# The softplus of a selective scan as one activation, and three of eight products with C on GpSimd

## What is computed

```
x, z = split(hidden @ W_in)                        # 1024 + 1024 features
x = silu(causal_conv4(x) + conv_b)
x_dbl = x @ W_x                                    # 64 + 16 + 16 columns: dt_raw, B, C
dt = softplus(x_dbl[..., :64] @ W_dt + b_dt)       # 224 x 1024 per sequence
h[t] = exp(dt[t] * A) * h[t-1] + (dt[t] * x[t]) * B[t]      # 16 states per feature
y[t] = sum over the 16 states of h[t] * C[t]
y = (y + x * D) * silu(z);  out = residual + y @ W_out
```

## Time and profile before

| | us |
|---|---|
| median of 3 runs (3502.21 to 3515.01) | 3507.85 |
| profiled execution, first to last instruction | 3514.3 |
| PE busy | 3186.9 (91%) |
| DVE busy | 2650.7 (75%) |
| ACT busy | 2396.1 (68%) |
| POOL busy | 1805.3 (51%) |

### The profile page before, as it was taken

One profiled execution on the slowest core, in us unless ns is written; L12 is line 12 of the kernel. 1 busy time (PEld: TensorE's weight loads), 2 busy tenths in 40 slices (PEclk: granted clock), 3 DMA queues, 4 the chain that ended last, 5 costly groups with the idle time before them and its releaser, 6 DMA issues. The chain is left out here.

```text
span 3514.3 us, 59833 instructions
## 1 busy us (share of the span) xinstructions
PE 3186.9 (91%) x20864; PEld 2223.5 (63%) x20864; DVE 2650.7 (75%) x4673; ACT 2396.1 (68%) x5339; POOL 1805.3 (51%) x1211
## 2 busy tenths in 40 slices
PE   5699889888889888988998899999999999899999
PEld 4566556665566556655665566666666666578887
DVE  2889999999999999999987576777777777523222
ACT  5778887778787887778774477776777677632222
POOL 2677887888787878888786100100000010055554
PEclk8899999999999999999999999999999999999999
DMA  5566666766677666666576121211211121120010
GB/s 164 154 180 183 185 167 164 199 185 163 156 193 192 164 161 184 177 183 158 157 201 182 53 71 49 83 55 47 75 64 47 52 81 66 43 77 25 27 46 24
DMA packets 286298, 425.03 MB, mean 121 GB/s; under 512 B 28753, under 2 KB 226129, under 8 KB 281394
## 3 DMA queue, kind: packets, MB, share of 16 engines
q1 hardware_dynamic: 278637, 411.44, 42.0%
q10 hardware_dynamic: 7365, 9.77, 1.0%
HBM read 320.12 MB, written 101.02 MB: 120 GB/s over the span
## 5 line engine op out<-in xcount | busy, mean ns | idle before, releaser
L811 POOL TENSOR_TENSOR a_hs<-a_rep,a_bmat 128x896 f32<-128x896 f32 x512 | 1061.5, 2097 | 294.6 <-PE a_yps L323 294.4
L443 ACT ACTIVATE a_states<-a_rep,a_a_neg 128x224 f32<-128x224 f32 x2048 | 793.7, 438 | 98.0 <-DVE a_hs L707 96.4
L700 DVE TENSOR_TENSOR_SCAN a_states<-a_states,a_hs 128x900 f32<-128x900 f32 x384 | 779.7, 2031 | 73.8 <-ACT a_states L443 58.5
L1424 DVE CUSTOM_DVE_ANT_0 b_sc<-sps,early_mask 112x375 f32<-112x375 f32 x1024 | 500.3, 545 | 171.7 <-PE sps L1171 162.1
L1311 ACT ACTIVATE b_sc<-b_sc,b_nmax 112x750 f32<-112x750 f32 x512 | 467.3, 913 | 2.5 <-DVE b_nmax L1430 2.5
L1185 PEld LDWEIGHTS b_tps<-ident,b_sc 112*125 112x125 f32 x3072 | 362.2, 191 | 157.4 <-issue 126.1
L1564 POOL TENSOR_SCALAR b_x_var<-mv 112x2 f32<-112x2 f32 x16 | 3.4, 214 | 857.4 <-DVE mv L1475 857.4
L345 PE MATMUL a_work<-early_scan_hT,w_in 128*128 128x224 f32 x2048 | 427.6, 364 | 10.0 <-issue 7.2
L345 PEld LDWEIGHTS a_work<-early_scan_hT,w_in 128*128 128x128 f32 x2048 | 397.9, 197 | 51.1 <-issue 43.4
L707 DVE TENSOR_TENSOR a_hs<-a_states,a_cmat 128x896 f32<-128x896 f32 x384 | 419.2, 1092 | 13.2
L1185 PE MATMUL b_tps<-ident,b_sc 112*125 112x112 f32 x3072 | 410.7, 283 | 16.3 <-DVE b_pT L1438 14.9
(11 more groups left out here) (199 smaller groups left out, 5012.4 us busy)
## 6 DMA issues: line engine op xcount, KB each, us to landing
a_rep<-du_scratch SPq DMA_DIRECT2D x512, 224.0 KB, 5.7
w_in<-W_in_dram SPq DMA_DIRECT2D x128, 512.0 KB, 4.4
du_scratch<-early_du SPq DMA_DIRECT2D x16, 1792.0 KB, 11.4
ctx<-ctxT_dram SPq DMA_DIRECT2D x48, 500.0 KB, 5.8
v_scratch<-kv_out SPq DMA_DIRECT2D x96, 250.0 KB
k_scratch<-kv_out SPq DMA_DIRECT2D x96, 250.0 KB, 4.4
b_keys<-k_scratch SPq DMA_DIRECT2D x8, 1500.0 KB, 9.2
b_v<-v_scratch SPq DMA_DIRECT2D x8, 1500.0 KB
```

Of the source, the lines that this page charges most:

```text
L443: e = act.activation(rows(states[:, g % DA, :])[:, q, 1:ROW], rep[tile % REPS][:, j, 0, :], ACT.Exp, scale=a_neg[:, g % SLOTS, q:q + 1])
L700: dve.tensor_tensor_scan(state if g % G4 else whole, state, whole, 0.0, ALU.mult, ALU.add).then_inc(S["scan"], 1)
L811: pool.tensor_tensor(hs[g % RING][:, :, 1:ROW], rep[tile % REPS][:, j, 1, :].unsqueeze(1).broadcast_to([P, Q, L]), bmat[b % 2][:], ALU.mul ...
L1424: dve.tensor_tensor_reduce(out=sc[buffer_of(block)][:, j, cols], in0=sps[0:TT, j, 0:HALF], in1=mask[:, block % 2, cols], scale=-1.0, scala ...
```

## The change

The softplus becomes one Softplus activation per pair of tiles, straight from PSUM into dt. VectorE's two passes, GpSimd's sum and six of the seven activation passes are gone. Softplus is in a table of its own, so the four activations stand together in one slot with a table load before and after them. GpSimd makes the product with C for three slots of eight (g % 8 of 0, 4 and 6) and VectorE for five; before it was two and six. The tables of slots move with it: the dt matmuls of a sequence in two pairs, at slots 18 and 21, the softplus at 21, `scale_x` at 22, `store_du` at 23, z one slot later, some of the key and value units shifted. `skip` no longer stands behind the softplus.

```diff
-            "silu_x": [-43], "x_dbl": [-42], "xd": [-41], "store_bc": [-41], "dt": spaced(-40, 1), "parts": spaced(-39, 1),
-            "series": spaced(-38, 1), "logs": spaced(-37, 1), "skip": [-32, -31], "spread": [-28], "dt_sum": [-30],
-            "silu_z": [-20], "u": [-28], "store_du": [-27]}
+            "silu_x": [-43], "x_dbl": [-42], "xd": [-41], "store_bc": [-41], "dt": [-40, -40, -40, -39],
+            "softplus": [-39, -39, -39, -39], "skip": [-42, -42], "spread": [-38], "silu_z": [-20], "u": [-38],
+            "store_du": [-37]}
...
-            "older_taps": spaced(-47, 4), "z": spaced(-47, 4), "keep_z": spaced(-46, 4), "residual": [-35], "silu_x": [-34],
-            "x_dbl": [-33], "xd": [-32], "store_bc": [-32], "dt": spaced(-30, 2), "parts": spaced(-29, 2),
-            "series": spaced(-28, 2), "logs": spaced(-27, 2), "skip": [-20, -19], "spread": [-19], "dt_sum": [-18],
-            "silu_z": [-16], "u": [-16], "store_du": [-15]}
+            "older_taps": spaced(-47, 4), "z": spaced(-46, 4), "keep_z": spaced(-45, 4), "residual": [-35], "silu_x": [-34],
+            "x_dbl": [-33], "xd": [-32], "store_bc": [-32], "dt": [-18, -18, -15, -15],
+            "softplus": [-15, -15, -15, -15], "skip": [-20, -19], "spread": [-19], "silu_z": [-11], "u": [-14],
+            "store_du": [-13]}
...
-        usual = (1, 3, 5, 12, 14, 18, 20, 22, 24, 26, 30)
+        usual = (1, 3, 5, 12, 13, 18, 20, 21, 24, 25, 29)
...
+        def pool_multiplies(g):
+            return g % (2 * G4) in (0, G4, G4 + 2)
...
             def sum_states(tile):
-                pe.wait_ge(S["hc"], (G4 - 1) * (tile + 1))
-                pe.wait_ge(S["hc_pool"], tile + 1)
+                pe.wait_ge(S["hc"], products(G4 * tile + G4 - 1))
+                pe.wait_ge(S["hc_pool"], pool_products(G4 * tile + G4 - 1))
...
             def dt_raw(b, pair):
-                bank = take_bank(("dt", b, pair), "part", PAIRS * b + pair + 1)
+                bank = take_bank(("dt", b, pair), "dt", PAIRS * b + pair + 1)
...
-                act.preload_act_table_set("natural_log_exp_and_others")
+                act.preload_act_table_set("natural_log_exp_and_others" if b else "softplus")
...
+            def softplus(b, pair):
+                act.wait_ge(S["dt_ps"], PAIRS * b + pair + 1)
                 act.wait_ge(S["xs"], 2 * (b + 1))
...
+                act.activation(dt[:, 2 * pair:2 * pair + 2, :], pair_of_tiles("dt", b, pair),
+                               ACT.Softplus).then_inc(S["dt"], 1)
+                if pair == PAIRS - 1:
+                    act.preload_act_table_set("natural_log_exp_and_others")
...
             def scale_x(b):
                 pool.wait_ge(S["skip"], 2 * (b + 1))
-                pool.wait_ge(S["dt"], b + 1)
+                pool.wait_ge(S["dt"], PAIRS * (b + 1))
...
-                if 0 <= slot - AHEAD < ALL and (slot - AHEAD) % G4 == 0:
-                    times_c(slot - AHEAD)
+                for g in (slot - AHEAD, slot - AHEAD + 1):
+                    if 0 <= g < ALL and pool_multiplies(g) and (g % G4 == 0) == (g == slot - AHEAD):
+                        times_c(g)
```

## The result

The changed kernel takes 3697.87 us (median; 3689.39 to 3699.57), the one before 3506.72 (median of four here; the table above has three of them): a ratio of 1.0537, 95% interval 1.0518 to 1.0555. It is slower by 191 us. The forecast was slower too, but by 88 us, and its range ended at 3645. The profiled span is 3696.2 us against 3514.3, 181.9 more. One execution of one kernel further down (softplus at slot 10, two products), its only profiled one, ran at a lower granted clock throughout, 0.83, and took 3732.71 us; no reading here rests on it.

A forecast was written before the change was run, and what follows sets the result against it. GpSimd's queue order and the late softplus before u were taken to hold TensorE's sums: 13 windows x 7.2 (4.8 walk, 2.4 clock) = +94, -9 prologue, +3 other windows gave +88, 3596 us; range 3498 to 3645.

The forecast's parts named there:

- the chain: Slots 20 to 24: late softplus and dt, then u, then queued GpSimd inputs and products before the sum at 24: 22.8 us.
- the clock term of the sum: TensorE's lower clock after waits: 2.4 us per window, bound 0 to 5, three places of which two are on the chain.
- the last window: Sequence 0's window and the last two hold other lists of units: +3 us together, between -10 and +15.
- the prologue: Before the first scan: without the passes u can start at about 48; gain -9 us, between -4 and -14.
- What bounds the kernel: DVE's work sets most of the pace, but GpSimd's order, not its share, already holds TensorE twice per window.
- The walk: Following TensorE's sums, one per four slots, by what ends last between them: 118.8 us per window against 114.0, +4.8.
- the recorded sum: 13 steady windows x 7.2 = +94, prologue -9, other windows +3: +88 us, added to the median: 3596.
- Softplus and table loads: At slot 21: Softplus priced as Exp, bounds 0.53 to 0.67 us; a table load 1.28 us, without the skill's 1.38 drain.
- (a): Rival: VectorE keeps the pace and the others' losses are slack; about -150 us, 3358; chance 0.10.
- (b): Rival: GpSimd sets the pace, dt complete early enough to cover its wait; window 107.6, about -99 us, 3409; chance 0.09.
- (c): Rival: gain and loss cancel if dt comes some 5 us earlier than walked; within 10 us of 3508; chance 0.07.
- (e): Rival: Softplus takes twice another pass at slot 21; +2 us per window, 30 us in all, 3626; chance 0.08.

The follow-up runs named there:

- GpSimd's order alone: Changed kernel with GpSimd's products with C one slot earlier in its queue and the gate at slot 10 instead of 8, no work added: 3583.12 us.
- The fill: Changed kernel with extra unread matmuls before TensorE's sums at slots 8, 16 and 24 and the third dt pair at 21: 3624.50 us.
- the run at slot 14: Changed kernel with the softplus at slot 14 instead of 21, dt matmuls at 12 and 14, u at 20, still three products of eight: 3586.27 us.

## Why the prediction was wrong, point by point

The direction and the chain were right, the size was not: +191 us for +88. The step that failed is the clock term of the sum, 2.4 us per window where the traces show about 7; two small terms, the last window and the prologue, were wrong as well.

**What bounds the kernel: right.** That GpSimd's order and not its share holds TensorE was read from the waits of 3.36 and 3.04 us, and the run with GpSimd's order alone showed it: 115 us. VectorE's 108 us a window, from which its 99 follow, are 106.4 by the earlier trace rows; no step of the walk uses them.

**The walk: right in its places and, but for the clock, within 0.3 us per stretch.** From the sums of one window after, starts at 1001.44, 1016.29, 1028.31, 1043.80, 1068.35, 1084.81 and on, and the medians over sequences 3 to 13, in us:

| slots | before, median | walk | after, this window | after, median |
|---|---|---|---|---|
| 8 to 12 | 19.2 | 12.2 | 14.9 | 14.4 |
| 12 to 16 | 10.9 | 11.7 | 12.0 | 12.0 |
| 16 to 20 | 17.1 | 14.5 | 15.5 | 16.9 |
| 20 to 24 | 12.9 | 22.8 | 24.6 | 23.3 |
| 24 to 28 | 14.7 | 14.8 | 16.5 | 16.2 |
| 28 to 32 | 14.7 | 14.8 | 14.7 | 14.7 |
| 0 to 4 | 12.3 | 11.5 | 11.8 | 11.8 |
| 4 to 8 | 12.9 | 16.5 | 16.8 | 16.8 |

The sum of the walk was 118.8, the window measured from the sum at 1001.44 to the next at 1128.15 is 126.7. Of the signs that the forecast named: the window of 119 to 124 us was 125.9. GpSimd's wait before u, forecast at 8 to 11 us, was 12.6 to 13.05. The wait before the sum at 24, forecast at 7, was 5.55, since the units before it were slow too; the one at 8 was 8.03, for 5 to 8. VectorE's idle share, forecast to go from 4% to 15%, went from 7% to 21%.

**The clock: the step that failed.** I took 2.4 us per window, with a bound of 5 for three places of which two count. All four stretches that came out clearly longer than the walk begin with, or hold, a wait followed by slow matmuls: 2.65 + 1.0 + 1.75 + 1.65, about 7 us in this window, and 5.6 to 7 in all of sequences 3 to 13. The third dt pair, whose wait of 2.7 us I had in the walk, wasn't among my places at all, and it lies on the chain to u. The fill showed that the term is real: 4.2 us of each window and 73 us in all, with one of its four places not covered. That is 125.9 against 121.2, 4.7 us x 14 = 66 of the 94 us by which the span's change was missed. With 7 us in its place the recorded sum would have given 13 x 11.8 - 9 + 3 = +147, 3655 us, which is still 43 below the measured time; the next two points hold 24 of that, and a fourteenth window at the full loss, where I counted 13, another 12.

**The last window: missed.** I took +3 with the first one. It is +19.6 behind the last gate. The run with the third product alone has +14.4 there (3581.6 - 1888.4 against 3514.3 - 1835.5 = 1678.8), the run with the Softplus alone +0.3. The stretch has three parts. From the gate to the next sum it is 12.0 us for 8.1, in both kernels with the third product in its old place: that is the product behind the gate again. From that sum to the last one it is 97.5 for 89.6 (96.3 with the third product alone, 90.6 with the Softplus alone, 91.8 with GpSimd's better order). So some 12 of the 19.6 us are the third product's, in a window without any softplus; the sums at 2009.77 and 2042.38 wait for it and are slow:

```profile
2009.77 2.39 PE L326 MATMUL a_yps<-a_hs,a_fold 128*32 128x224 f32 x32 [3.82 <-POOL a_hs L786]
...
2042.38 3.21 PE L326 MATMUL a_yps<-a_hs,a_fold 128*32 128x224 f32 x32 [3.21 <-POOL a_hs L786]
```

The other 7.9 us lie behind the last sum, 1588.9 for 1581.0, mostly in attention and feed-forward, which the change doesn't touch. That part took 1580.5 to 1588.9 us in the traces of the other kernels too, without order, so its cause is open and it may be no effect at all.

**The prologue: the start of u right, the gain -2 for -9.** u began at 47.02, as said (48), 15.4 us earlier than in the earlier trace rows, but the first scan only at 83.06 for 85.00:

```profile
60.03 8.79 PE L348 MATMUL a_work<-early_scan_hT,w_in 128*128 128x224 f32 x32 [7.66 <-issue]
```

The last two z units start at 60.03 (59.92 before), though the softplus is over earlier; ScalarE's silu of z, the next sequence's norm and the first decays come behind them. In the kernel before, SP issues weights for such units at 56.39, ahead of the store of u at 66.42; in the changed one it stores u at 51.03 and issues the weights at 51.42, right behind. From 50 to 60 us the DMA engines are then busy throughout (share 0.95 to 1.05), and one of the 16 loads of weights up to 110 us takes 9.2 us to land (the profile doesn't say which), where the median is 3.6. So the earlier store most likely held up the weights; this is read from the trace, and no run tried another order.

**Softplus and table loads: right.** 0.54 us for a Softplus and 1.28 us for a table load, with the activation 0.02 us behind it. The 1.38 us of drain that the Trainium skill (ScalarE: Activation LUTs, What ACT_TABLE_LOAD costs) adds don't show here either.

**The rivals.** (a), VectorE's pace, and (b), dt in time, fell: their windows of 105 and 107.6 us stand in none of the 13 traces compared here, and the lowest is 110.0. Rival (c)'s condition, an earlier dt, gave 112 of the 191 us back in the run at slot 14. (e) fell with the row.

**What was not seen:** that the two parts of the change cost far more together than apart. The cost of the third product is 71 us with the old softplus, 216 with the changed kernel's slots, 125 with GpSimd's better order, and 3 with that order and the softplus at 10. I priced the change as one chain and so had the meeting in the sum, but never asked for each part alone, where the Softplus was a gain of 25 us. And VectorE's relief, 4.4 us a window, never showed up as a gain: at best the third product cost 3 us, which is within the noise. Why the softplus at slot 10 doesn't beat that at 21 is located, in the stretch from 8 to 12, but by the trace with three products; which of the steps that meet there sets it, no run isolates.

## What to carry to other kernels

In a program of in-order engines that meet at one point, price an added instruction by what stands between it and that point in its own queue, not by the engine's share: the same product cost 3 or 216 us, by what stood around it. Write down for each meeting point which instruction of each engine releases it, and move short, awaited ones ahead of long ones that nobody waits for (the gate at slot 10 instead of 8, products one slot earlier). And try each half of a change alone: here one was a gain of 25 us that the other hid.

## What the runs showed of the hardware

TensorE's clock can be a price of a wait, also of a short one. In the changed kernel, behind waits of 2.7, 5.6 and 8.0 us, the granted clock was at its lower level (1.2 of 2.4 GHz, 0.50 in the rows of the window shown), behind one of 3.2 us it was 0.54, and the work took up to twice as long: a sum of 1.74 us took 3.22, two dt pairs 3.36 for 1.68. It is uneven: in one kernel the sum behind 3.23 us took 1.73 and in another, behind the same wait, 3.05; and in the kernel with GpSimd's better order the sum at 24 took 1.74 behind 3.97 us in some windows and 3.21 behind 3.47 in others. I had expected a third of it. Filling the waits with 128x64 matmuls (0.11 us per instruction, two for each matmul) raised the granted clock of the scan from 0.90 to 0.98 and gave 73 us where TensorE was late for all the others, and nothing that the times can show where VectorE was.
